# First four attention steps with the query-key projections one block ahead

## The chip, the cores and the metric

The kernel runs on one core of one Trainium2 chip. The metric is device time in microseconds (us) of one launch; "TensorE", "VectorE", "ScalarE" and "GpSimd" are PE, DVE, ACT and POOL in the rows of the profile, SP is the engine whose queue issues most transfers, and PEld is TensorE's loading of weights.

## The reference

One transformer layer on a sequence of 4096 tokens, width 256: banded attention with 16 heads of 16 columns, then a feed-forward block with binarised weights, each with a residual and a layer norm.

```python
q = _l2norm(proj(Wq)); k = _l2norm(proj(Wk)); v = proj(Wv)
attn = jnp.einsum('bhqd,bhkd->bhqk', q, k)
mask = (rel < 0) | (rel >= WINDOW)            # rel = key position - query position, WINDOW = 128
alibi = -jnp.abs(rel) * slopes[:, None, None]
attn = jax.nn.softmax(attn + where(mask, -1e30, alibi), axis=-1)
out = einsum('bhqk,bhkd->bhqd', attn, v) @ Wo
x = _layernorm(x + out)
h = gelu(x @ (alpha1 * sign(w1)).T + b1)      # alpha = mean |w| of a row
x = _layernorm(x + h @ (alpha2 * sign(w2)).T + b2)
```

## The kernel before

The tokens are cut into 32 blocks of 128. Attention works through the blocks in steps, one per block; step i handles the keys of block i, whose queries are those of blocks i and i-1. The work of one block passes through all engines, and every engine has its own program, written out by hand in order; semaphores tie them together. An engine works strictly in its written order, so a waiting instruction holds all that is behind it. Steps 0 to 3 are written out one by one (this is the head of the program, and all that is changed), steps 4 to 23 are a loop of four steps a turn, and the last eight steps run into the feed-forward block.

The names used here, each with its line in the rows:

- **qk(n)**: TensorE projects queries and keys of block n into a bank of PSUM (L430; block 0 at L499), float32, four passes of 512 columns. It waits until block n-2, which used the same bank, is normalised (`qkn_done`).
- **sq(n)** squares on ScalarE (L638), **sums(n)** on VectorE (L923), **seed(n)** on VectorE (L836); **norm(i)** is the pair logarithm and exponential on ScalarE (L643, L645) for block i+3; then a round of three short operations (L841, L843, L845) and the normalising of the rows (L946) on VectorE.
- **high(n)** on ScalarE (L652, L655) writes the float16 high halves of block n into `parts[n % 2]`; the low halves are subtracted on GpSimd (L1338, L1340); **double(n)** copies the query halves (on ScalarE, L665, in most steps; L898 on VectorE for the first blocks).
- **T(n)**: SP's queue issues a DMA transpose of `parts` into slot n % 4 of `qkT` (L284). high(n+2) overwrites the same half of `parts` and so waits until T(n) has landed.
- **S(i,c)**: TensorE's scores of step i, chunk c of four (L398). **E(i,c)**: ScalarE's exponential of that chunk (L685). S(i,c) needs E of two chunks earlier, since the chunks take two pairs of banks in turn.
- **cuts**: four per step on GpSimd (L1320), which set masked weights to zero.
- **v(n)**: TensorE's projection of the values (L441), then their fading by VectorE (L915). It is written into the bank that also holds the small normaliser parts of VectorE, so it waits for `newton` (a finished round) and `onorm_done` (a finished scaling of sums).
- **W(q)**: TensorE's weighted sums of block q (L420), in step q+2. VectorE turns them (L852), takes the reciprocal (L858) and scales (L861, `onorm_done`), and TensorE projects them with `wo` (L450).

TensorE's program opens with warm-up products of a constant (L492, `WARM`), and has two more such stretches in the head: 14 before step 0 (`WARM_AGAIN`) and 6 in step 1 (`WARM_BETWEEN`).

Of the kernel before, what the change touches and what calls it, by code (L numbers as in the profile page):

```python
# [15 lines left out]
P = 128  # L16
D = 256
# [28 lines left out]
WARM_AGAIN = 14  # L46

WARM_BETWEEN = 6


# [67 lines left out]
def build(nc, x, xT, wqkvT, woT, w1, w1T, b1c, w2T, b2, out):  # L118
    with ExitStack() as ctx:
# [81 lines left out]

        rden_in_psum = ps[:, VO, D + 192:D + 192 + H]
        parts_in_psum = tuple(ps[:, VO, D + 64 * n:D + 64 * n + 2 * H + 1] for n in range(3))

        def in_psum(i, next3):

            return next3 and (not isinstance(i, int) or i >= 0)
# [59 lines left out]
        def _(sp):  # L267
# [6 lines left out]
            def turn_parts(n, s):  # L274
# [6 lines left out]
                if isinstance(n, int) and n < 2:  # L281
                    sp.wait_ge(first_low, n + 1)
# [4 lines left out]
            for n in range(DC):  # L287
                sp.dma_start(wqkv[:, n, 0:2 * D], wqkvT[:, n, 0:2 * D]).then_inc(wqk_in[n], 16)
                sp.dma_start(xt[:, n], xT[n]).then_inc(x_in[n], 16)
            for n in range(DC, XS):  # L290
# [3 lines left out]
            load_block(XS, 0)  # L294
            turn_parts(0, 0)
            turn_parts(1, 1)
            turn_parts(2, 2)
            load_block(XS + 1, 1)
            load_block(XS + 2, 2)
            turn_parts(3, 3)  # L300
            sp.dma_start(wo[:], woT).then_inc(wo_in, 16)
            load_block(XS + 3, 3)
            for n in range(2):
                sp.dma_start(resid[:, n, :], x[n]).then_inc(first_resid[0], 16)
            turn_parts(XS, 0)
            for n in range(2, XS):
                sp.dma_start(resid[:, n, :], x[n]).then_inc(first_resid[1], 16)
# [64 lines left out]
        def _(pe):  # L372
# [187 lines left out]
            def means():  # L560

                pe.wait_ge(w2_summed, 3)
                pe.wait_ge(v_ready, NB)
                nc.tensor.matmul(mean_at, mean_ones[:], w2_sum[:], start=True, stop=True).then_inc(means_done, 1)
# [68 lines left out]
        def _(act):  # L633
# [34 lines left out]
            def step(i, slot, next2=True, next3=True, ln=True, both=True, norm=True, high_first=False,  # L668
                     squares_first=False, doubled=True, before_rows=None, amid=None, tail=None):
                par = slot % 2  # L670
                own, near = OWN_AT[slot], NEAR_AT[par]
                at = slice(near, own + 1, own - near)

                def exps(c):
                    act.wait_ge(s_done, i * NC + c + 1)
                    if c == 0:
                        count(act, pv_done, i - 2)
                    banks = ps[:, SC + 2 * (c % 2):SC + 2 * (c % 2) + 2, :]
                    if both:
                        to = prob[:, at, CH * c:CH * c + CH, :].rearrange("p s h q -> p h s q")  # L680
                        scored = banks.rearrange("p b (t s q) -> p (b t) s q", t=2, s=2)
                    else:
                        to = prob[:, own, CH * c:CH * c + CH, :]
                        scored = banks.rearrange("p b (t q) -> p (b t) q", t=2)[:, :, P:2 * P]
                    nc.scalar.activation(to, scored, ACT.Exp, scale=QK_SCALE ** -2).then_inc(exp_done, 1)  # L685

                if high_first:
                    high_halves(i + 2, par)
                exps(0)
                exps(1)  # L690
                if next2 and not high_first and not squares_first:
# [5 lines left out]
                if squares_first:  # L697
                    high_halves(i + 2, par)
                if amid:
                    amid()  # L700
                exps(2)
                exps(3)
                if norm and (next3 or ln):
                    norm_of(i, next3, ln)
                if next2 and doubled:
# [19 lines left out]

            nc.scalar.preload_act_table_set("natural_log_exp_and_others")
# [106 lines left out]
        def _(dve):  # L833
# [67 lines left out]
            def split_keys(n):  # L901

                dve.wait_ge(hi_done, n + 1)
                nc.vector.tensor_tensor(parts[:, n, H:2 * H, 2:4, :],
                                        qkn[:, n, D:2 * D].rearrange("p (h d) -> p h d", d=HD).unsqueeze(2).to_broadcast(
                                            [P, H, 2, HD]),
                                        parts[:, n, H:2 * H, 0:2, :], ALU.subtract).then_inc(first_low, 1)
                double(n, n)

            def fade_values(n, slot):  # L910

                dve.wait_ge(v_done, n + 1)
                count(dve, pv_done, n - 3)
                v = ps[:, VO, 0:D].rearrange("p (h d) -> p h d", d=HD)
# [115 lines left out]
            sums_of(1)  # L1030
# [459 lines left out]
```

## Time and profile before

| | us |
|---|---|
| median of 3 runs | 356.14 (355.18 to 356.33) |
| the profiled execution, its own time | 355.92 |
| its span, first to last instruction | 354.2 |
| TensorE busy | 333.9 (94%) |
| ScalarE busy | 295.4 (83%) |
| VectorE busy | 288.7 (81%) |
| GpSimd busy | 266.8 (75%) |

The span leaves out 1.72 us of the profiled execution's time. Busy shares are averages over stages that differ; the head, from 0 to 40.14 us, is the part that the change rewrites. "Idle before" in a row is the time that an engine stood still ahead of the row, with the instruction that ended it.

### The profile page before, as it was taken

The page shows a single profiled execution, that of the slowest core. Times are in us where ns is not written, and L with a number is a line of the kernel's source. Part 1 is how long each engine was busy: PE and PEld are TensorE (multiplying, and loading weights), DVE is VectorE, ACT ScalarE, POOL GpSimd, SP SyncE. Part 2 cuts the span into 40 slices and gives each one's busy share as a digit, 9 for nine tenths or more (in the row PEclk, how much of TensorE's full clock was granted, in tenths as well). Part 3 has the DMA queues.
Part 4 walks back from the last instruction along what each step waited for, and adds up shares of the span by engine and source line. Part 5 has one row for each costly group of instructions (what it writes and reads, how often), then busy time and mean ns, then how long its engine had stood idle before and what let it go on. Part 6 is the DMA issues. An engine that isn't in the chain of part 4 may idle for free.

```text
span 354.2 us, 12284 instructions
## 1 busy us (share of the span) xinstructions
PE 333.9 (94%) x4269; PEld 227.1 (64%) x4269; DVE 288.7 (81%) x763; ACT 295.4 (83%) x496; POOL 266.8 (75%) x314
## 2 busy tenths in 40 slices
PE   8798998999999999999998979898999999999991
PEld 6555675667666676676675657665766666676781
DVE  5875789789889989989987866988778788787785
ACT  2489988889989899899898996878788888897843
POOL 1149998888988998998899986856685765766343
PEclk9999999999999999999999998999999999999998
DMA  7577854555555565686775583012320721413113
GB/s 227 130 140 174 192 125 92 120 119 119 119 118 118 107 135 128 148 176 150 160 173 125 101 165 60 3 20 44 59 57 6 121 83 37 118 59 60 59 61 119
DMA packets 99489, 38.32 MB, mean 108 GB/s; under 512 B 84736, under 2 KB 98432, under 8 KB 99328
## 3 DMA queue, kind: packets, MB, share of 16 engines
q1 hardware_dynamic: 99456, 37.89, 48.3%
q8 instruction: 19, 0.31, 0.4%
q14 instruction: 14, 0.11, 0.1%
HBM read 12.72 MB, written 4.19 MB: 48 GB/s over the span
## 4 chain that ended last, share of the span: by engine, by line
PE 69%; DVE 10%; issue 6%; ACT 5%; DMA 4%; POOL 3%; SPq 1%; DVEq 1%; POOLq 0%; ACTq 0%
PE ps L551 14%; PE ps L581 13%; PE ps L430 11%; PE ps L420 11%; PE ps L441 6%; PE ps L398 6%; PE ps L450 5%; ACT prob L685 2%; DMA yT<-yparts 2%; DMA qkT<-parts 1%; SPq L284 1%; PE ps L492 1%; DMA resid<-in_x 1%; DVE otok L861 1%; POOL prob L1320 1%
## 5 line engine op out<-in xcount | busy, mean ns | idle before, releaser
L1320 POOL TENSOR_SCALAR_AFFINE_SELECT prob<-prob 128x1024 f32<-128x1024 f32 x126 | 133.7, 1094 | 5.9 <-ACT prob L685 5.7
L685 ACT ACTIVATE prob<-ps 128x1024 f32<-128x1024 f32 (+1 forms) x128 | 121.8, 1004 | 11.4 <-PE ps L398 11.1
L551 PE MATMUL ps<-yT,sgn 128*128 128x512 f16 x256 | 61.0, 379 | 2.5 <-DMA yT<-yparts 2.5
L430 PE MATMUL ps<-wqkv,xt 128*128 128x512 f32 x124 | 61.4, 617 | 1.2 <-DVE qkn L946 1.1
L420 PE MATMUL ps<-prob,faded 128*17 128x128 f32 x2016 | 61.2, 273 | 0.6 <-POOL prob L1320 0.6
L755 ACT ACTIVATE ps<-ps,bias,alpha 128x512 f32<-128x512 f32 x64 | 47.9, 749 | 15.3 <-PE ps L551 12.1
L420 PEld LDWEIGHTS ps<-prob,faded 128*17 128x17 f32 x2016 | 52.3, 97 | 6.5 <-issue 3.7
L1388 POOL TENSOR_TENSOR resid<-z,resid 128x256 f32 (+1 forms) x31 | 22.4, 724 | 29.4 <-DVE z L1148 29.4
L551 PEld LDWEIGHTS ps<-yT,sgn 128*128 128x128 f16 x256 | 24.7, 98 | 26.1 <-issue 3.1
L398 PE MATMUL ps<-qkT 64*64 64x192 f16 (+3 forms) x1024 | 36.8, 255 | 4.7 <-DMA qkT<-parts 2.2
L398 PEld LDWEIGHTS ps<-qkT 64*64 64x64 f16 x1024 | 20.9, 106 | 25.4 <-issue 25.1
L1340 POOL TENSOR_TENSOR parts<-qkn,parts 128x512 f16<-128x512 f32 x30 | 35.7, 1189 | 0.0
L441 PE MATMUL ps<-wqkv,xt 128*128 128x256 f32 x128 | 34.7, 395 | 0.8 <-DVE otok L861 0.8
L430 PEld LDWEIGHTS ps<-wqkv,xt 128*128 128x128 f32 x124 | 21.1, 189 | 21.5 <-issue 18.2
L1338 POOL TENSOR_TENSOR parts<-qkn,parts 128x256 f16<-128x256 f32 x30 | 20.3, 677 | 19.0 <-ACT parts L655 18.9
L450 PEld LDWEIGHTS ps<-wo,oT 128*128 128x128 f32 x112 | 21.4, 192 | 14.5 <-issue 12.8
L581 PE MATMUL ps<-sgn,w 128*128 128x256 f16 x256 | 30.6, 273 | 0.0
L450 PE MATMUL ps<-wo,oT 128*128 128x256 f32 x112 | 29.4, 386 | 0.6 <-DVE turned L852 0.6
L1370 POOL TENSOR_TENSOR yparts<-resid,yparts 128x256 f16<-128x256 f32 (+1 forms) x32 | 21.5, 689 | 11.0 <-ACT yparts L749 11.0
L581 PEld LDWEIGHTS ps<-sgn,w 128*128 128x128 f16 x256 | 25.0, 98 | 6.3
L441 PEld LDWEIGHTS ps<-wqkv,xt 128*128 128x128 f32 x128 | 23.6, 194 | 7.6 <-issue 4.3
L581 PE MATMUL ps<-sgn,prob 128*128 128x256 f16 x240 | 28.3, 273 | 0.0
(114 smaller groups left out, 558.6 us busy)
## 6 DMA issues: line engine op xcount, KB each, us to landing
xt<-in_xT SPq DMA_DIRECT2D x32, 128.0 KB, 2.3
resid<-in_x SPq DMA_DIRECT2D x32, 128.0 KB, 2.3
out_dram<-resid SPq DMA_DIRECT2D x7, 512.0 KB, 2.9
w<-in_w2T SPq DMA_DIRECT2D x1, 1024.0 KB, 8.2
w<-in_w1T SPq DMA_DIRECT2D x4, 256.0 KB, 3.3
w_nat<-in_w SPq DMA_DIRECT2D x4, 256.0 KB, 4.3
wqkv<-in_wqkvT SPq DMA_DIRECT2D x3, 256.0 KB, 4.1
qkT<-parts SPq DMA_TRANSPOSE x32, 4.3
```

The source lines that it names most:

```text
L398: mm = nc.tensor.matmul(ps[keys, SC + 2 * (c % 2) + hp, 2 * P * t + first:2 * P * t + last], qkT[row, H // 2 + 2 * c + t, slot, keys], moving,
L420: mm = nc.tensor.matmul(ps[32 * m:32 * m + HD + 1, OT, P * c:P * c + P], v, p, start=(n == 0), stop=(n == 1 or not near))
L430: mm = nc.tensor.matmul(ps[:, QK[slot % 2], :], xt[:, slot, k, :], wqkv[:, k, 0:2 * D], start=(k == 0), stop=(k == DC - 1))
L441: mm = nc.tensor.matmul(ps[:, VO, 0:D], xt[:, slot, k, :], wqkv[:, k, 2 * D:3 * D], start=(k == 0), stop=(k == DC - 1))
L450: mm = nc.tensor.matmul(ps[:, OT, D * par:D * par + D], oT[:, par, k, :], wo[:, k, :], start=(k == 0), stop=(k == DC - 1))
L551: mm = nc.tensor.matmul(ps[:, bank, :], sgn1[:, c, P * k:P * k + P], yT[:, par, a, c, :, :], start=(m == 0), stop=(m == 2 * DC - 1))
L581: mm = nc.tensor.matmul(ps[:, banks[b], 0:D], hid[par][:, a, k, P * b:P * b + P], sgn2[:, k, :], start=(m == 0), stop=(m == 2 * HC - 1))
L685: nc.scalar.activation(to, scored, ACT.Exp, scale=QK_SCALE ** -2).then_inc(exp_done, 1)
L755: nc.scalar.activation(bank, bank, ACT.Gelu, bias=bias1[:, k:k + 1], scale=alpha1[:, k:k + 1]).then_inc(gelu_done, 1)
L1320: return nc.gpsimd.affine_select(out=at, in_=at, compare_op=ALU.is_ge, fill=0.0, base=-near, pattern=[[0, 2 * CH], [1 if near else -1, P]] ...
L1340: nc.gpsimd.tensor_tensor(parts[:, par, H:2 * H, 2:4, :], src[:, H:2 * H, :].unsqueeze(2).to_broadcast([P, H, 2, HD]), parts[:, par, H:2 * ...
L1388: nc.gpsimd.tensor_tensor(resid[:, m, :], z[:, b, :], resid[:, m, :], ALU.add).then_inc(zsum, 1)
```

## The change

Only the head is changed. (1) TensorE does qk(3), v(1) and v(2) ahead of step 0 in place of 14 warm-up products, and the 6 products of step 1 are gone. The values of blocks 1 and 2 go into the bank of the weighted sums (`first_values`), which is free then. In steps 0, 1 and 2 TensorE does qk(4), qk(5), qk(6), a block ahead of before, and step 3 has none. (2) v(3) is in step 2 ahead of W(0), and v(4) in step 3, between the second and third chunk of the scores. (3) ScalarE does high(i+3) and norm(i+1) in step i, and nothing but exponentials in step 3. (4) Blocks 2 to 5 are doubled on VectorE. (5) The seeds of blocks 1 and 2 go to PSUM in place of SBUF. (6) The first block's transfer and the second half of the query-key weights are issued by ScalarE's queue. (7) On SP's queue the loads of blocks 5 and 6 stand between the transposes, each ahead of the next one. (8) The sums of `w2` come in four pieces.

```diff
-            def project_v(n, slot):
+            def first_value(n):
+                pe.wait_ge(x_in[n], 16)
+                for k in range(DC):
+                    mm = nc.tensor.matmul(first_values[n], xt[:, n, k, :], wqkv[:, k, 2 * D:3 * D],
+                                          start=(k == 0), stop=(k == DC - 1))
+                mm.then_inc(v_done, 1)
+            def project_v(n, slot, ahead=0):
...
-                if not isinstance(n, int) or 2 <= n < NB - 1:
-                    pe.wait_ge(newton, norm_base(n - 2, True) + NORM_OPS)
+                if not isinstance(n, int) or n < NB - 1:
+                    pe.wait_ge(newton, norm_base(n - 2 + ahead, True) + NORM_OPS)
                 count(pe, onorm_done, n - 3)
...
-            project_v(0, 0)
+            first_value(0)
             project_qk(2, 2)
-            pe.wait_ge(id_made, 2)
+            pe.wait_ge(consts, 1)
+            first_value(1)
+            project_qk(3, 3)
+            first_value(2)
             pe.wait_ge(consts, 2)
-            keep_warm(WARM_AGAIN, SC)
-            step(0, 0, out=False, pv=False, both=False, early=True)
-            step(1, 1, out=False, pv=False, behind=lambda: keep_warm(WARM_BETWEEN, OT))
-            step(2, 2, out=False, early=True)
-            step(3, 3, out=False, early=True)
+            for i in range(2):
+                for c in (0, 1):
+                    scores(i, c, i, i, i > 0)
+                project_qk(i + 4, i)
+                for c in (2, 3):
+                    scores(i, c, i, i, i > 0)
+            for c in (0, 1):
+                scores(2, c, 0, 2, True)
+            project_qk(6, 2)
+            for c in (2, 3):
+                scores(2, c, 0, 2, True)
+            project_v(3, 3, ahead=1)
+            for c in range(NC):
+                weighted_sum(0, c, 0)
+            for c in (0, 1):
+                scores(3, c, 1, 3, True)
+            project_v(4, 0, ahead=1)
+            for c in (2, 3):
+                scores(3, c, 1, 3, True)
+            for c in range(NC):
+                weighted_sum(1, c, 1)
...
+            act.dma_start(xt[:, 0], xT[0]).then_inc(x_in[0], 16)
+            act.dma_start(wqkv[:, 1, 0:2 * D], wqkvT[:, 1, 0:2 * D]).then_inc(wqk_in[1], 16)
             nc.scalar.preload_act_table_set("natural_log_exp_and_others")
...
-            step(0, 0, ln=False, both=False, high_first=True, doubled=False)
-            step(1, 1, ln=False, squares_first=True)
-            step(2, 2, ln=False, squares_first=True)
-            step(3, 3, ln=False, squares_first=True)
+            squares(3, 1)
+            high_halves(2, 0, first=True)
+            norm_of(0, True, False)
+            for i in range(3):
+                for c in (0, 1):
+                    exps(i, c, i, i > 0)
+                squares(i + 4, i % 2)
+                high_halves(i + 3, 1 - i % 2)
+                for c in (2, 3):
+                    exps(i, c, i, i > 0)
+                norm_of(i + 1, True, False)
+            for c in range(NC):
+                exps(3, c, 3)
...
             seeds_of(6, False)
+            turn_sums(0)
+            round_of(3, True, False)
+            normalise_rows(6, 0)
             scale_sums(0, 0)
```

TensorE, between block 2's projection and the first scores (L492 are the warm-up products; L422 is qk, L430 the new early values, L390 the scores). Before:

```order
L430 MATMUL ps<-wqkv,xt 128x512 [waits qkn_done,x_in_2]
L430 MATMUL ps<-wqkv,xt 128x512
L492 MATMUL ps<-mean_ones 128x128 [waits consts,id_made]
L492 MATMUL ps<-mean_ones 128x128 x13
L398 MATMUL ps<-qkT 64x64 [waits qk_in_even,consts]
```

And of the change:

```order
L422 MATMUL ps<-wqkv,xt 128x512 [waits qkn_done,x_in_2]
L422 MATMUL ps<-wqkv,xt 128x512
L430 MATMUL ps<-wqkv,xt 128x256 [waits x_in_1,consts]
L430 MATMUL ps<-wqkv,xt 128x256
L422 MATMUL ps<-wqkv,xt 128x512 [waits qkn_done,x_in_3]
L422 MATMUL ps<-wqkv,xt 128x512
L430 MATMUL ps<-wqkv,xt 128x256 [waits x_in_2]
L430 MATMUL ps<-wqkv,xt 128x256
L390 MATMUL ps<-qkT 64x64 [waits qk_in_even,consts]
```

One query-key and two value projections stand where the warm-up products stood.

TensorE in step 3, from its second chunk of scores to the weighted sums W(1). Before (L430 is qk(6), L441 is v(4), L420 is W(1)):

```order
L398 MATMUL ps<-qkT 64x192 [waits exp_done,consts]
L398 MATMUL ps<-qkT 64x192 x7
L430 MATMUL ps<-wqkv,xt 128x512 [waits qkn_done,x_in_2]
L430 MATMUL ps<-wqkv,xt 128x512
L398 MATMUL ps<-qkT 64x192 [waits exp_done,consts]
L398 MATMUL ps<-qkT 64x192 x7
L398 MATMUL ps<-qkT 64x192 [waits exp_done,consts]
L398 MATMUL ps<-qkT 64x192 x7
L441 MATMUL ps<-wqkv,xt 128x256 [waits onorm_done,newton,v_ready]
L441 MATMUL ps<-wqkv,xt 128x256
L420 MATMUL ps<-prob,faded 17x128 [waits cut_ready,sums_turned,v_ready]
L420 MATMUL ps<-prob,faded 17x128 x15
```

And of the change (L390 scores, L441 v(4), L412 W(1)):

```order
L390 MATMUL ps<-qkT 64x192 [waits exp_done,consts]
L390 MATMUL ps<-qkT 64x192 x7
L441 MATMUL ps<-wqkv,xt 128x256 [waits onorm_done,newton,v_ready]
L441 MATMUL ps<-wqkv,xt 128x256
L390 MATMUL ps<-qkT 64x192 [waits exp_done,consts]
L390 MATMUL ps<-qkT 64x192 x7
L390 MATMUL ps<-qkT 64x192 [waits exp_done,consts]
L390 MATMUL ps<-qkT 64x192 x7
L412 MATMUL ps<-prob,faded 17x128 [waits cut_ready,sums_turned,v_ready]
L412 MATMUL ps<-prob,faded 17x128 x15
```

v(4), with its wait for the scaling of block 0's sums, has moved ahead of the third and fourth chunk of the scores, and qk(6) is no longer there.

SP's queue around the first transposes, of the change (L268 and L269 load a block, L281 is a transpose; before, the three transposes stood together and the loads of blocks 5 and 6 behind them):

```order
L268 DMA xt<-in_xT 128x256 [waits v_done]
L269 DMA resid<-in_x 128x256
L281 DMA_TRANSPOSE qkT<-parts 128x16x128 [waits parts_ready,first_low,wv_in]
L268 DMA xt<-in_xT 128x256 [waits v_done]
L269 DMA resid<-in_x 128x256
L281 DMA_TRANSPOSE qkT<-parts 128x16x128 [waits parts_ready,first_low,wv_in]
```

Two loads now stand between T(0) and T(1), and two more between T(1) and T(2).

## Rows read from the trace of the kernel before

**Rows 1.** Windows by stage: length, then each engine's busy us and instruction count.

```profile
17.85:40.14 22.29, 21.27 (x301) 12.63 (x301) 14.89 (x32) 20.83 (x39) 17.67 (x19) 1.00 0.76 168
40.14:169.39 129.25, 127.45 (x2077) 86.93 (x2078) 114.17 (x311) 117.20 (x196) 117.96 (x118) 1.00 0.60 129
```

**Rows 2.** Chain that ended last, in order of time: start, length, what.

```profile
13.33 4.38 DMA qkT<-parts
...
34.66 1.91 PE ps L430 x4
...
37.17 1.06 PE ps L441 x4
38.23 1.87 PE ps L420 x64
...
40.14 0.63 PE ps L398 x16
...
59.74 1.02 issue
```

**Rows 3.** Timeline of TensorE up to step 0: start, length, engine, line, operation.

```profile
5.84 0.28 PEld L499 LDWEIGHTS ps<-wqkv,xt 128*128 128x128 f32 x1 [0.81 <-DMA wqkv<-in_wqkvT]
...
6.40 1.30 PE L499 MATMUL ps<-wqkv,xt 128*128 128x512 f32 x2
...
13.13 3.29 PE L492 MATMUL ps<-mean_ones 128*128 128x128 f32 x28
17.85 0.36 PE L398 MATMUL ps<-qkT 64*64 64x64 f16 x14 [1.43 <-DMA qkT<-parts]
```

**Rows 4.** Timeline of ScalarE, the first exponentials and step 2.

```profile
18.70 1.06 ACT L685 ACTIVATE prob<-ps 128x512 f32<-128x512 f32 x2
...
28.86 1.92 ACT L685 ACTIVATE prob<-ps 128x1024 f32<-128x1024 f32 x2
30.73 0.60 ACT L638 ACTIVATE sq<-ps 128x512 f32<-128x512 f32 x1
31.23 0.41 ACT L652 ACTIVATE parts<-qkn 128x256 f16<-128x256 f32 x1
...
32.05 1.93 ACT L685 ACTIVATE prob<-ps 128x1024 f32<-128x1024 f32 x2
33.86 0.20 ACT L643 ACTIVATE lnx<-ps 128x32 f32<-128x32 f32 x1
34.10 0.23 ACT L645 ACTIVATE rnorm<-lnx 128x32 f32<-128x32 f32 x1
34.23 0.61 ACT L665 ACTIVATE parts<-parts 128x512 f16<-128x512 f16 x1
34.75 1.92 ACT L685 ACTIVATE prob<-ps 128x1024 f32<-128x1024 f32 x2
```

**Rows 5.** SP's queue, and transposes' landing times, 12 to 30 and 30 to 200 us.

```profile
16.64 1.86 SPq L284 DMA_TRANSPOSE qkT<-parts  x1
...
23.80 1.15 SPq L271 DMA_DIRECT2D xt<-in_xT  x1
...
DMA to landing us min/median/max: 4.3/4.5/4.7
...
DMA to landing us min/median/max: 4.2/4.3/6.0
```

**Rows 6.** Timeline of VectorE: two seeds, and the turning and scaling of W(0).

```profile
11.83 0.61 DVE L836 TENSOR_SCALAR half<-ss 128x32 f32<-128x32 f32 x1
...
26.67 0.18 DVE L836 TENSOR_SCALAR ps<-ss 128x32 f32<-128x32 f32 x1
...
34.28 0.72 DVE L852 STREAM_TRANSPOSE turned<-ps 128x512 f32<-128x512 f32 x1 [1.11 <-PE ps L420]
...
36.48 0.42 DVE L861 TENSOR_TENSOR otok<-turned,ps 128x256 f32<-128x256 f32 x1
```

**Rows 7.** TensorE after its longest idle time, and window with its granted clock.

```profile
210.56 1.02 PE L551 MATMUL ps<-yT,sgn 128*128 128x512 f16 x4 [2.51 <-DMA yT<-yparts]
...
212.00:213.50 1.50, 1.50 (x5) 0.50 0.29 55
```

More of the change, by code:

```diff
@@ L44 @@
 WARM = 8
-WARM_AGAIN = 14
-WARM_BETWEEN = 6
+HEAD = 3
 OWN_AT, NEAR_AT = (2, 3, 4, 5), (0, 1)
@@ L205, in in_psum @@
         def in_psum(i, next3):
-            return next3 and (not isinstance(i, int) or i >= 0)
+            return next3 and (not isinstance(i, int) or i > -HEAD)
         def root_parts(i, next3):
@@ L666, in double @@
                                      ACT.Copy).then_inc(parts_ready, 1)
-            def step(i, slot, next2=True, next3=True, ln=True, both=True, norm=True, high_first=False,
-                     squares_first=False, doubled=True, before_rows=None, amid=None, tail=None):
-                par = slot % 2
[L671 to L691, printed above, removed]
@@ new lines, in exps @@
+            def exps(i, c, slot, both=True):
+                own, near = OWN_AT[slot], NEAR_AT[slot % 2]
+                at = slice(near, own + 1, own - near)
+                act.wait_ge(s_done, i * NC + c + 1)
+                if c == 0:
+                    count(act, pv_done, i - 2)
+                banks = ps[:, SC + 2 * (c % 2):SC + 2 * (c % 2) + 2, :]
+                if both:
+                    to = prob[:, at, CH * c:CH * c + CH, :].rearrange("p s h q -> p h s q")
+                    scored = banks.rearrange("p b (t s q) -> p (b t) s q", t=2, s=2)
+                else:
+                    to = prob[:, own, CH * c:CH * c + CH, :]
+                    scored = banks.rearrange("p b (t q) -> p (b t) q", t=2)[:, :, P:2 * P]
+                nc.scalar.activation(to, scored, ACT.Exp, scale=QK_SCALE ** -2).then_inc(exp_done, 1)
@@ L696, in step @@
                     before_rows()
-                if squares_first:
-                    high_halves(i + 2, par)
                 if amid:
                     amid()
-                exps(2)
-                exps(3)
-                if norm and (next3 or ln):
+                exps(i, 2, slot)
+                exps(i, 3, slot)
+                if next3 or ln:
                     norm_of(i, next3, ln)
-                if next2 and doubled:
+                if next2:
                     double(i + 2, par)
@@ L1342, in low_halves, with step @@
                                         parts[:, par, H:2 * H, 0:2, :], ALU.subtract).then_inc(lo_done, 1)
-            def step(i, slot, next2=True, both=True, low_at=1, behind=None):
+            def step(i, slot, next2=True, both=True, low_at=1, ahead=0, behind=None):
                 for pair in range(NC // 2):
                     if next2 and pair == low_at:
-                        low_halves(i + 2, slot % 2)
+                        low_halves(i + 2 + ahead, (slot + ahead) % 2)
                     cut_pair(i, pair, slot, both)
@@ L1350, in step @@
                     behind()
-            for n in range(2):
+            for n in range(HEAD):
                 pool.wait_ge(first_high, n + 1)
-                nc.gpsimd.tensor_tensor(parts[:, n, 0:H, 1, :], qkn[:, n, 0:D].rearrange("p (h d) -> p h d", d=HD),
-                                        parts[:, n, 0:H, 0, :], ALU.subtract).then_inc(lo_done, 1)
-            step(0, 0, both=False, low_at=0)
-            step(1, 1, low_at=0)
-            for n in range(2, 5):
-                step(n, n % XS, low_at=0)
+                nc.gpsimd.tensor_tensor(parts[:, n % 2, 0:H, 1, :], qkn[:, n % 2, 0:D].rearrange("p (h d) -> p h d", d=HD),
+                                        parts[:, n % 2, 0:H, 0, :], ALU.subtract).then_inc(lo_done, 1)
+            step(0, 0, both=False, ahead=1)
+            step(1, 1, ahead=1)
+            step(2, 2, ahead=1)
+            step(3, 3, next2=False)
+            step(4, 0, low_at=0)
             with pool.Fori(0, (NB - 12) // XS) as t:
```

69 lines of the change are left out of this document (38 added, 31 removed).

## The prediction

> **What bounds the kernel now.** I read the windows by stage first, then the chain of work that ended last, then each engine's timeline over the head. The windows show two full engines in the head: from the first scores at 17.85 to step 4 at 40.14, TensorE is busy 21.27 of 22.29 us and ScalarE 20.83; in the loop behind it TensorE is busy 127.45 of 129.25 us [rows 1]. The chain runs through TensorE there, line after line without a gap [rows 2]. So the loop keeps TensorE's pace, and the head is worth what it moves the start of step 4, which stands at 40.14. Everything behind is the same program; a shift of step 4 passes to the end.
>
> ScalarE explains the head's pace: in step 2 it starts a pair of exponentials at 28.86 and, without a pause, the next step's at 34.75. By differences of starts a pair of E is 1.87 (1.81 the second), sq 0.50, high 0.82 (31.23 to 32.05), norm 0.37 (33.86 to 34.23) and double 0.52 [rows 4]: 5.89 a step. TensorE's own list for a step is also near 5.9: qk(6) 1.91, v(4) 1.06, W(1) 1.87, and the 0.60 left between the first two for a pair of scores [rows 2]; two such pairs and that make 6.0, less where a pair overlaps its neighbours.
>
> **The change part by part.**
>
> *Early projections.* qk(3), v(1), v(2) are 1.91 + 2 x 1.06 = 4.0 us, and replace warm-up products that began at 13.13; the first transpose lands at 13.33 + 4.38 = 17.71 [rows 2, 3]. There are 4.6 us; qk(3) must wait for block 1's normalising (I take 14.6, an estimate: 1.4 us behind the start of the warm-up products, whose place v(1) takes), so the last ends near 17.5. It fits, with 0.2 to spare, and costs nothing; if it ran over, step 0 would start later by as much. It takes 4 us and 20 warm-up products out of TensorE behind 17.85, which makes about 15 of its 21 us needed. TensorE then no longer bounds the head, ScalarE does, if nothing stops it.
>
> *First loads on two queues.* The second weight half lands at 5.84, while the pass that uses it starts at 6.40, in the engine's own pace [rows 3]. An earlier landing is worth 0; a later first load costs at most one issue, under 0.5. I take 0. The Trainium skill (DMA: Bandwidth & Descriptors, Issuing engines are not separate DMA queues) says that both queues end on the same transfer engines and only issue time is saved; by it too the edit is worth 0, at most the issue time, and that is hidden.
>
> *Seeds to PSUM.* A seed into SBUF took 0.61, one into PSUM 0.18 [rows 6]; twice 0.43 on VectorE's opening chain. I expect 0.15 to 0.3 of it at block 2's normalising. T(1), next, takes it back.
>
> *Loads between transposes.* A transpose holds SP's queue 1.86, the load behind one takes 1.15, and a landing comes 4.3 to 4.7 after issue [rows 5]. T(0) issued at 13.2 (13.33, less the seed's gain), the two loads (1.15 + 0.4) end near 16.8, so T(1) is issued 0.2 later than its 16.64 and behind 256 KB of loads; I take its landing at 21.3, with 20.9 (no loss) and 22.0 as ends. high(3) is now ahead of E(0,2) and waits for T(1).
>
> *ScalarE's walk.* norm(0) is now ahead of E(0,0), which goes from 18.70 to 18.9. E pair to 19.9; sq(4) waits for qk(4), 20.1; high(3) at 21.35 (T(1)); E(0,2) 22.2; norm(1) 23.2; E(1,0) 23.55; sq(5) waits for qk(5) (S(1,1) behind E(0,3), then 1.91), 25.6; high(4) 26.1; E(1,2) 26.95; norm(2) 28.75; E(2,0) 29.15; sq(6) 31.25, again behind qk(6); high(5) 31.75; E(2,2) 32.55; norm(3) 34.4 to 34.85. So step 2's exponentials start at 29.15 where they started at 28.86: ScalarE has a block more of preparation behind it, and no lead. The lead should be paid out in step 3, which has only four E, 3.75 in place of 5.89.
>
> *The step's new wait.* TensorE: qk(6) 29.3 to 31.2, S(2,2) and S(2,3), v(3), then W(0) 32.9 to 34.8, S(3,0) and S(3,1) to 35.2. Then v(4), which waits for W(0) to be scaled. From the start of the turning to the end of the scaling was 34.28 to 36.90, 2.62 us, with the round and the normalising of a block between [rows 6]; the same rows stand between them now. Turned at 34.87, scaled at 37.5, v(4) from 37.6 to 38.7. Before, TensorE had qk(6) and S(3,2), S(3,3) to do in that time; now these chunks stand behind v(4), and E(3,2), ready for 36.7, starts at 39.1. Then a pair of S, for which I take 0.5, W(1) 39.15 to 41.0, and S(4,0) at 41.05 against 40.14: **+0.9 us**. What is late next is only step 4 itself; ScalarE ends E(3,3) at 41.1 and is not late for it.
>
> *Doubling on VectorE.* ScalarE saves 0.52 in steps 1 to 3. VectorE has the time: it is busy 14.89 of 22.29 [rows 1]; blocks 3 and 4 are doubled while it waits for squares. If VectorE had no room, each copy would cost up to its 0.6. GpSimd's list is the same in sum, and its cuts of block 1 and 2 are ready before W(0) and W(1) by my count, the second by 1.5 us. The sums of w2 in four pieces lie in VectorE's pauses: 0.
>
> **Sum.** Profiled execution 355.92 (span 354.2) + 0.9 = 356.8; its time is 0.22 below the median 356.14, so against the runs it is 357.0. The bounds: T(1) on time and no wait of sq behind qk gives back at most 1.35 of ScalarE's path, which puts S(4,0) at 39.7 (-0.45, 355.7); T(1) at 22.0 gives +1.6 (357.7).
>
> **The rivals.**
>
> *Wait not met.* The scaling of W(0) is done before S(3,1) ends, as it would be if norm(3) came 1.7 us earlier than in my walk. Then v(4) is free, S(3,2) comes at once, and step 4 follows ScalarE: norm(3) plus four E, S(4,0) near 37.9, 2.2 us earlier: 353.9. For it speaks the 4 us taken from TensorE; against it that ScalarE has only 1.4 us of pauses in my walk. It decides at W(0)'s turning: under 33.2 us it is this one.
>
> *Clock.* My walk leaves TensorE idle from 20.5 to 22.7, 26.2 to 28.0 and 35.2 to 37.6 (1.8 to 2.4 us), with the warm-up products gone. In the trace, 2.51 us without products at 208 were followed by a granted clock of 0.50, 1.2 GHz, at 212 [rows 7]; the 1.43 us ahead of step 0 [rows 3] by none. A stretch at half clock of about 3 us loses half of it: +1.6 more, 358.6. The Trainium skill (TensorE: Matmul & The Clock Gate, Part 1) has the throttled state as the default and activity as what releases it, and warns of kernels whose waits let the clock fall again and again; by that page warm-up products are not free to remove, and the sum would be this rival's. The trace agrees in kind.
>
> *Transposes late.* T(1) or T(2) lands in up to 6.0, the longest seen [rows 5], since loads stand ahead of them: high(3) at 22.8, all +1.5: 358.0.
>
> *Stall behind goes.* Step 7's scores waited 1.02 at 59.74 [rows 2] for a transpose, the one of 6.0. With another phase of the transfers it may vanish: 357.0 - 1.0 = 356.0.
>
> **How the numbers follow.** Mine 0.50, wait not met 0.15, clock 0.15, late transposes 0.10, stall gone 0.10. A measurement of this kernel tells about 0.3%, 1.07 us, from no change: below 355.07 faster, above 357.21 slower. My case's value is close below that edge; a third of it lies above. Slower: 0.17 + 0.15 + 0.08 = 0.40; faster: 0.15 and 0.03 of the last, 0.18; same 0.42. The range runs from 354.7 to 358.6: it leaves out most of the first rival and the far end of the clock, takes in both bounds of T(1). My own case's range is 355.7 to 357.7.
>
> **What would show it.** Right: step 2's E starts between 28.5 and 29.6; a TensorE wait of about 2 us in front of v(4) ended by the scaling (VectorE's `otok`), and a ScalarE wait of 2 us in front of E(3,2); S(4,0) at 40.7 to 41.4. Wrong: no such wait; high(3) not ended by T(1); passes of qk of double length behind a pause; or a time that moves while S(4,0) stands where I say, which would put the cause into the loop.

## The result

| | before | change |
|---|---|---|
| median, us | 356.23 (355.18 to 356.41, 6 runs) | 358.31 (354.96 to 358.88, 6 runs) |
| ratio | | 1.0066, 95% interval 1.0037 to 1.0094 |
| profiled execution, its own time | 355.92 | 354.96 |
| its span | 354.2 | 352.8 |

The change is slower by 0.7%. The profiled execution of the change is the fastest of its six; the other five lie between 358.0 and 358.9. Its profile is read here for what happens in the head, and a second one (`after_again`, below) is nearer to the usual execution.

TensorE in the head of the change (timeline: start, length, engine, line, operation, and idle time before with what ended it; L422 is qk, L430 an early value, L390 scores, L441 v, L412 W, L492 warm-up):

```profile
4.50 1.96 PE L499 MATMUL ps<-wqkv,xt 128*128 128x512 f32 x4
6.29 1.88 PE L422 MATMUL ps<-wqkv,xt 128*128 128x512 f32 x4
...
16.82 0.42 PE L390 MATMUL ps<-qkT 64*64 64x64 f16 x16 [0.65 <-DMA qkT<-parts]
...
21.57 0.85 PE L390 MATMUL ps<-qkT 64*64 64x192 f16 x16 [2.08 <-ACT prob L701]
22.35 1.98 PE L422 MATMUL ps<-wqkv,xt 128*128 128x512 f32 x4
...
26.85 0.36 PE L390 MATMUL ps<-qkT 64*64 64x192 f16 x8 [2.06 <-ACT prob L701]
...
28.05 3.68 PE L422 MATMUL ps<-wqkv,xt 128*128 128x512 f32 x4
...
37.95 1.60 PE L441 MATMUL ps<-wqkv,xt 128*128 128x256 f32 x4 [2.38 <-DVE otok L886]
...
40.26 2.67 PE L412 MATMUL ps<-prob,faded 128*17 128x128 f32 x64
42.87 0.63 PE L390 MATMUL ps<-qkT 64*64 64x256 f16 x16
```

Step 4's first scores, S(4,0), start at 42.87, where they started at 40.14 [rows 2]. TensorE's stretches that matter for this are the three with an idle time of 2 us ahead of them, and what follows each. The three idle times of the prediction's walk are there, 2.08, 2.06 and 2.38 us, and behind two of them the same operations take longer: qk(6) takes 3.68 where qk(5) takes 1.98, v(4) 1.60 where an undisturbed one takes 1.1, W(1) 2.67 against 1.94 in the timeline of before. The windows of TensorE say why (length, busy us and count, granted clock, DMA share, GB/s):

```profile
17.85:40.14 22.29, 15.10 (x196) 0.88 0.67 145
...
27.50:29.00 1.50, 1.24 (x10) 0.72 0.82 208
29.00:30.50 1.50, 1.50 (x3) 0.50 0.09 24
...
32.00:38.00 6.00, 3.62 (x97) 1.00 0.74 166
38.00:39.50 1.50, 1.50 (x8) 0.64 0.02 5
39.50:41.00 1.50, 1.50 (x33) 0.50 0.26 68
41.00:42.50 1.50, 1.50 (x48) 0.73 0.85 197
```

TensorE was busy 21.27 us of the first window before [rows 1], and is busy 15.10 now: the work did leave. But the granted clock in the head, 1.00 before, falls twice to 0.50, the lower of the two levels (1.2 GHz).

ScalarE over the same time (L701 exponentials, L657 squares):

```profile
20.01 0.42 ACT L671 ACTIVATE parts<-qkn 128x256 f16<-128x256 f32 x1 [0.22 <-DVE qkn L973]
...
27.87 1.92 ACT L701 ACTIVATE prob<-ps 128x1024 f32<-128x1024 f32 x2
31.77 0.60 ACT L657 ACTIVATE sq<-ps 128x512 f32<-128x512 f32 x1 [1.98 <-PE ps L422]
...
35.46 1.94 ACT L701 ACTIVATE prob<-ps 128x1024 f32<-128x1024 f32 x2
40.07 1.94 ACT L701 ACTIVATE prob<-ps 128x1024 f32<-128x1024 f32 x2 [2.67 <-PE ps L390]
```

The slow qk(6) reaches ScalarE as a wait of 1.98 ahead of sq(6), and the wait ahead of v(4) as one of 2.67 ahead of E(3,2). high(3), at 20.01, was released by the normalising, not by the landing of T(1).

Although step 4 comes 2.73 later, this execution's span is 1.4 shorter than that of before. To compare executions I split each time into four: the opening up to the start of qk(1), the head from there to S(4,0), the rest up to the end of the span, and the time outside the span.

| profiled execution | opening | head | rest | outside | own time |
|---|---|---|---|---|---|
| before | 7.54 | 32.60 | 314.06 | 1.72 | 355.92 |
| change | 6.29 | 36.58 | 309.93 | 2.16 | 354.96 |
| change, again | 6.90 | 37.98 | 309.92 | 2.27 | 357.07 |

The opening differs because the first pass over the weights takes a different time in each execution: L499's four products took 3.01 in the profile of before and 1.96 in this one. The profile's clock column reads 1.00 there, so a lower clock in the opening would be a guess from these lengths alone. The difference does not belong to the change: qk(1) starts at 7.54, 7.53 and 6.67 in the three profiles of the kernel before and its variants, and between 6.29 and 7.64 in those of the change and its own. The head is 3.98 longer. The rest is 4.13 shorter, and the views of both name most of that. The list of TensorE's waits between 45 and 160 us has, for the kernel before (engine, line, releaser: us in total, times, longest):

```profile
PE ps L398 <- issue: 1.0, 1, 1.0
PE ps L441 <- DVE otok L861: 0.8, 2, 0.4
```

and nothing at all for the change. The stall at 59.74 [rows 2] and two waits for the scaling of sums are gone: 1.8 us. The other piece is the first transpose of the feed-forward block, which the prediction had used only as a sample of an idle TensorE [rows 7]. In the profile of the change:

```profile
209.84 1.02 PE L570 MATMUL ps<-yT,sgn 128*128 128x512 f16 x4 [0.67 <-DMA yT<-yparts]
```

That wait was 2.51 [rows 7] and is 0.67; the transfer lands 4.7 us after its issue instead of 6.4, which is another 1.8. No slow stretch follows either: from this product to the next weighted sums it is 3.13 us in place of 4.76. The pieces named so far come to 3.6 of the 4.13, so that of these 1.6 us only 0.5 are left at the end; where the other 1.1 are lost again was not traced.

### The profile page after: what moved, and what is told of

The parts are those of the page before. It is cut to its first block, busy times and chain, and to the rows that moved or that the text cites. A ratio compares the mean times of both kernels' runs of the same rounds, so it can differ in the third digit from the quotient of the medians.

```text
span 352.8 us, 12203 instructions
## 1 busy us (share of the span) xinstructions
PE 330.2 (94%) x4229; PEld 222.1 (63%) x4229; DVE 291.2 (83%) x768; ACT 294.0 (83%) x493; POOL 265.5 (75%) x313
## 4 chain that ended last, share of the span: by engine, by line
PE 73%; DVE 9%; ACT 6%; issue 4%; POOL 3%; DMA 3%; DVEq 0%; POOLq 0%; ACTq 0%; SPq 0%
PE ps L570 15%; PE ps L600 13%; PE ps L412 12%; PE ps L422 12%; PE ps L390 6%; PE ps L441 6%; PE ps L450 5%; ACT prob L701 3%; DMA yT<-yparts 1%; DMA qkT<-parts 1%; POOL prob L1355 1%; ACT parts L674 1%; PE ps L492 1%; DVE turned L877 1%; POOL parts L1375 1%
## 5 line engine op out<-in xcount | busy, mean ns | idle before, releaser
L701 ACT ACTIVATE prob<-ps 128x1024 f32<-128x1024 f32 (+1 forms) x128 | 121.7, 1004 | 10.6 <-PE ps L390 10.1
L422 PE MATMUL ps<-wqkv,xt 128*128 128x512 f32 x124 | 63.0, 632 | 1.5 <-DVE qkn L973 1.5
L412 PE MATMUL ps<-prob,faded 128*17 128x128 f32 x2016 | 62.2, 275 | 0.1
L412 PEld LDWEIGHTS ps<-prob,faded 128*17 128x17 f32 x2016 | 52.8, 98 | 6.3 <-issue 3.0
L1424 POOL TENSOR_TENSOR resid<-z,resid 128x256 f32 (+1 forms) x31 | 22.4, 725 | 29.6 <-DVE z L1183 29.6
L390 PE MATMUL ps<-qkT 64*64 64x192 f16 (+3 forms) x1024 | 37.0, 256 | 7.5 <-ACT prob L701 6.0
L390 PEld LDWEIGHTS ps<-qkT 64*64 64x64 f16 x1024 | 21.1, 106 | 29.1 <-issue 29.1
L422 PEld LDWEIGHTS ps<-wqkv,xt 128*128 128x128 f32 x124 | 21.5, 192 | 22.3 <-issue 18.9
L1375 POOL TENSOR_TENSOR parts<-qkn,parts 128x512 f16<-128x512 f32 x29 | 34.3, 1183 | 0.0
L441 PE MATMUL ps<-wqkv,xt 128*128 128x256 f32 x116 | 31.2, 392 | 2.4 <-DVE otok L886 2.4
L1373 POOL TENSOR_TENSOR parts<-qkn,parts 128x256 f16<-128x256 f32 x29 | 19.5, 672 | 15.7 <-ACT parts L674 15.4
L877 DVE STREAM_TRANSPOSE turned<-ps 128x512 f32<-128x512 f32 x32 | 22.9, 717 | 5.9 <-PE ps L412 5.6
```

The source lines that it names most:

```text
L390: mm = nc.tensor.matmul(ps[keys, SC + 2 * (c % 2) + hp, 2 * P * t + first:2 * P * t + last], qkT[row, H // 2 + 2 * c + t, slot, keys], moving,
L412: mm = nc.tensor.matmul(ps[32 * m:32 * m + HD + 1, OT, P * c:P * c + P], v, p, start=(n == 0), stop=(n == 1 or not near))
L422: mm = nc.tensor.matmul(ps[:, QK[slot % 2], :], xt[:, slot, k, :], wqkv[:, k, 0:2 * D], start=(k == 0), stop=(k == DC - 1))
L441: mm = nc.tensor.matmul(ps[:, VO, 0:D], xt[:, slot, k, :], wqkv[:, k, 2 * D:3 * D], start=(k == 0), stop=(k == DC - 1))
L877: nc.vector.transpose(turned[:].rearrange("p b d -> p (b d)"), ps[:, OT, :]).then_inc(sums_turned, 1)
L1375: nc.gpsimd.tensor_tensor(parts[:, par, H:2 * H, 2:4, :], src[:, H:2 * H, :].unsqueeze(2).to_broadcast([P, H, 2, HD]), parts[:, par, H:2 * ...
```

## The experiments

Eleven runs of ten kernels follow (`fill_again` repeats `fill`, and `after_again` the change), each with the kernel before beside it on the same chip; the medians of before were 355.45, 355.57 and 355.86 in the three sets. "Fillings" are warm-up products of a constant, written into a bank of PSUM that is free at that time; the rows count two matmuls to a product.

**`fill`, `fill_again`: TensorE busy in the three gaps**, by six, eight and nine products.

```diff
                 for c in (2, 3):
                     scores(i, c, i, i, i > 0)
+                pe.wait_ge(qkn_done, i + 4)
+                keep_warm((6, 8)[i], QK[1 - i])
...
+            pe.wait_ge(qkn_done, 6)
+            keep_warm(9, QK[1])
             project_v(4, 0, ahead=1)
```

> The changed kernel with warm-up products put into TensorE's three idle stretches of the head: 6 behind S(0,3), 8 behind S(1,3), 9 ahead of v(4). Theory (the clock): the two drops to 0.50 in the head go, qk(6) takes 1.98 in place of 3.68 and v(4) to W(1) 3.5 in place of 5.1; S(4,0) comes at 39.5 to 41.1 in place of 42.87, and the median falls by 2 to 3.3 from 358.3, to 355 to 356.3. Rival (the order of v(4), or the transfers, cost the time and the clock costs nothing): the products only fill idle time, median 358.3 again, within 0.5.

Measured: 354.93 (353.67 to 355.36, 12 runs), ratio 0.9984 (0.9969 to 0.9998). Repeated in the third set:

> The change with the three fillings of warm-up products a second time, as the ground for the next two. If the fillings give back what the lower clock cost, it stands where it stood, at 354.9, 0.2% under the kernel before, with the first scores of step 4 near 40.2. If that value came from a lucky phase of the transfers, it comes out near 355.7, where its neighbours stood.

Measured: 354.87 (353.65 to 355.32, 11 runs), ratio 0.9968 (0.9954 to 0.9981). TensorE in the profile of `fill_again`:

```profile
6.46 1.88 PE L422 MATMUL ps<-wqkv,xt 128*128 128x512 f32 x4
...
20.20 1.60 PE L492 MATMUL ps<-mean_ones 128*128 128x128 f32 x12 [0.53 <-DVE qkn L977]
...
25.07 2.05 PE L492 MATMUL ps<-mean_ones 128*128 128x128 f32 x16
...
28.40 1.98 PE L422 MATMUL ps<-wqkv,xt 128*128 128x512 f32 x4
...
34.16 2.27 PE L492 MATMUL ps<-mean_ones 128*128 128x128 f32 x18
36.61 1.10 PE L441 MATMUL ps<-wqkv,xt 128*128 128x256 f32 x4 [0.17 <-DVE otok L890]
...
39.96 0.63 PE L390 MATMUL ps<-qkT 64*64 64x256 f16 x16
```

The warm-up products do no work of the kernel and every wait for data is still there, yet qk(6) is back at 1.98 and v(4) at 1.10, and the granted clock is 1.00 from 14 to 45 us in both profiles. The head is 33.50 (33.35 in `fill`). So of the change's head, 36.58 and 37.98, 3.1 to 4.6 us were the lower clock, and against before's 32.60 there remain 0.75 and 0.90. Of that the time gets 3.3, in part because the wait for the feed-forward block's transpose is 2.2 again in both profiles with fillings, where the change has 0.7.

This does not rest on single profiles. The record gives every execution's mean granted clock: 0.976 to 0.979 in eleven of the twelve executions of the change and 0.985 in the fast one that was profiled first, against 0.990 to 0.994 in all 23 with the three fillings.

**`fill12`: the first two gaps filled, not the third.** The diff is that of `fill` without its last two lines.

> The changed kernel with warm-up products in the first two idle stretches only (6 behind S(0,3), 8 behind S(1,3)), none ahead of v(4). If each idle stretch of 2 us or more loses the clock by itself: the drop behind v(4) stays and costs 1.6, median 1.3 to 1.9 above the kernel with all three fillings (354.93). If the drops come from the sum of idle time in the head: no drop left, the same as with all three.

Measured: 357.11 (355.6 to 359.1, 12 runs), ratio 1.0056 (1.0033 to 1.0079). The gap ahead of v(4) alone, 2.38 us, is followed by a slow stretch:

```profile
37.44 1.95 PE L441 MATMUL ps<-wqkv,xt 128*128 128x256 f32 x4 [2.38 <-DVE otok L888]
...
40.09 2.33 PE L412 MATMUL ps<-prob,faded 128*17 128x128 f32 x64
42.36 0.63 PE L390 MATMUL ps<-qkT 64*64 64x256 f16 x16
```

The median is 2.2 above that of `fill`, where 1.3 to 1.9 was expected of a fall that stays. The head (34.89) shows 1.4 to 1.5 of it; behind step 4 this profile has waits of 0.8 and 0.7 in the loop that `fill` has not. The median also stands between two groups: six executions took 355.6 to 356.6 and six 357.6 to 359.1, and three of the slower six, the profiled one among them, have no lower mean clock (0.990) than the faster (0.988 to 0.989). So only the head's 1.4 to 1.5 is shown to be the clock.

**`after_again`: the change once more**, for a profile that isn't the fastest run.

> The changed kernel once more, beside the others of this set, for a second profile and its spread: 357.5 to 359, with clock drops in the head; if the first profiled execution (354.96) was the rule, 355.

Measured: 358.12 (357.07 to 358.72, 6 runs), ratio 1.008 (1.0059 to 1.0101). TensorE:

```profile
22.28 1.02 PE L390 MATMUL ps<-qkT 64*64 64x192 f16 x16 [2.17 <-ACT prob L701]
23.23 3.42 PE L422 MATMUL ps<-wqkv,xt 128*128 128x512 f32 x4
...
30.54 3.78 PE L422 MATMUL ps<-wqkv,xt 128*128 128x512 f32 x4
...
41.52 1.10 PE L441 MATMUL ps<-wqkv,xt 128*128 128x256 f32 x4 [2.38 <-DVE otok L886]
...
44.88 0.63 PE L390 MATMUL ps<-qkT 64*64 64x256 f16 x16
```

Here the first gap has its slow stretch too, and the third has none. Two of the three gaps are followed by one in each of the two profiles, not the same two; those hit behind the first or second cost a whole qk at half clock. With a later opening as well (6.90 against 6.29) this is 2.0 us of span above the first profile. It is the fastest of its six executions, but its mean clock, 0.979, is that of the others (0.976 to 0.979). By these profiles and the two of `fill`, one slow stretch costs the head 1.4 to 3 us, since what stands behind the qk can be slow too, as v(3) with 1.79 here.

**`v4last`, `fill_v4last`: the wait for the scaling out of the way.** v(4) moves behind W(1); in the second with the fillings (4 products ahead of S(3,2) in place of 9 ahead of v(4)).

```diff
             for c in (0, 1):
                 scores(3, c, 1, 3, True)
-            project_v(4, 0, ahead=1)
             for c in (2, 3):
                 scores(3, c, 1, 3, True)
             for c in range(NC):
                 weighted_sum(1, c, 1)
+            project_v(4, 0, ahead=1)
```

> The changed kernel with v(4) moved behind W(1), nothing else. Theory (v(4)'s wait for the scaling of W(0) holds the scores behind it): TensorE's wait of 2.4 and ScalarE's of 2.7 in step 3 go, S(4,0) comes 1.5 to 2.5 earlier than 42.87, and with the idle stretch the second drop of the clock may go too: median 355 to 356.8. Rival (the clock alone is the loss, TensorE waits for exponentials and cuts anyway): S(4,0) within 0.5 of 42.87, median 358 within 0.5.

Measured: 357.72 (357.17 to 358.47, 6 runs), ratio 1.0067 (1.0048 to 1.0087): by the ratios no faster than the change, and not the 355 to 356.8 that the theory wanted. S(4,0) starts at 44.46, not earlier than 42.87.

> Both: warm-up products in the first two idle stretches and 4 ahead of S(3,2), and v(4) behind W(1). If clock and wait are two separate losses: S(4,0) at 37.5 to 39, median 353 to 354.5, below the kernel before. If they are one loss seen twice: the same median as the better of the two alone.

Measured: 355.72 (355.13 to 357.02, 12 runs), ratio 1.0019 (1.0005 to 1.0032). Expected were 353 to 354.5 if clock and wait are two separate losses, and the median of the better of the two alone if they are one; it came out 0.8 above `fill`. The wait for `otok` is gone in the head of both. `v4last` leaves other gaps, and the clock falls behind them: W(1), behind idle times of 1.05 and 0.56, takes 3.59. With fillings the head is 32.87, 0.5 to 0.6 shorter than with the wait, and no shorter than before; the rest of its span, 312.6, is longer than that of `fill` (311.3; 312.3 in `fill_again`), and has waits of 0.4 and 0.3 in the loop. TensorE in `fill_v4last`:

```profile
37.45 1.94 PE L412 MATMUL ps<-prob,faded 128*17 128x128 f32 x64
39.32 1.13 PE L441 MATMUL ps<-wqkv,xt 128*128 128x256 f32 x4
40.38 0.63 PE L390 MATMUL ps<-qkT 64*64 64x256 f16 x16
```

v(4) can't start before the scaling (36.6 in `fill_again`), and W(1) and one or the other chunk of the scores can't either, since they follow ScalarE. So 3 us of TensorE's work stand between that moment and S(4,0) in both orders, and the work taken from TensorE earlier leaves idle time that neither order fills. That is argued from the rows, not shown; an order with v(4)'s bank freed was not tried.

**`before_nofill`: the kernel before without its warm-up products in the head.**

```diff
             pe.wait_ge(consts, 2)
-            keep_warm(WARM_AGAIN, SC)
             step(0, 0, out=False, pv=False, both=False, early=True)
-            step(1, 1, out=False, pv=False, behind=lambda: keep_warm(WARM_BETWEEN, OT))
+            step(1, 1, out=False, pv=False)
```

> The kernel before without its 14 and 6 warm-up products in the head. Theory (idle TensorE loses its clock, products are what kept it in the head): a granted clock of 0.50 appears between 14 and 35 us, 0.5 to 3.5 us slower than before. Rival (the kernel before has too little idle time in its head for that): within 0.5 of before, and the clock stays 1.00 in the head.

Measured: 356.0 (353.63 to 356.85, 12 runs), ratio 1.0011 (0.9993 to 1.0028). TensorE:

```profile
16.98 0.64 PE L398 MATMUL ps<-qkT 64*64 64x64 f16 x16 [4.54 <-DMA qkT<-parts]
17.55 3.78 PE L430 MATMUL ps<-wqkv,xt 128*128 128x512 f32 x4
```

The same thing happens to the old order: 4.54 us idle, then qk(3) at half clock; the granted clock is 0.50 from 16 to 20. Its head is 35.08, 2.5 longer than with the products. The median is not apart from before's (0.5 above it, with an interval that takes in no change), at the low end of the 0.5 to 3.5 expected. The profiled execution took 354.21 and is the second fastest of its twelve; ten of the others have a mean clock of 0.974 to 0.982, lower than its 0.986. In it the rest of the span is 310.65, nearly as short as the change's: the stall at 59.74 is gone and the wait for the feed-forward block's transpose is 0.70, while the waits for the scaling of sums are not (1.1 us in the loop).

**`before_two_queues`, `fill_one_queue`: the first loads.** The edit of ScalarE's queue put alone into the kernel before, and taken out of `fill`.

```diff
+            act.dma_start(xt[:, 0], xT[0]).then_inc(x_in[0], 16)
+            act.dma_start(wqkv[:, 1, 0:2 * D], wqkvT[:, 1, 0:2 * D]).then_inc(wqk_in[1], 16)
```

> The kernel before with only its first loads on two queues. As above: 0 to 0.4 slower if nothing is gained inside the span, 0.3 to 0.8 faster if the second weight half is what qk(0) waits for.

Measured: 355.97 (354.8 to 356.48, 12 runs), ratio 1.0005 (0.999 to 1.002), qk(1) at 7.53 and a head of 32.65, against 7.54 and 32.60.

> The changed kernel with all three fillings, but with the first loads all on SP's queue as before. If the two queues are worth nothing at the start: median as with all three fillings, within 0.3, or 0.4 faster, since the time outside the span is 2.2 with ScalarE's queue and 1.7 without. If they let the first projection start earlier: 0.3 to 0.8 slower.

Measured: 355.72 (355.25 to 357.22, 12 runs), ratio 1.0015 (1.0 to 1.0029). That is 0.8 above `fill`, the size that the second theory names; but its qk(1), at 7.13, stands within the spread of the openings, so that an earlier first projection is not shown to be the cause. Its profile is of the slowest of the twelve executions (357.22) and has a late transpose. SP's queue, then ScalarE's high(4):

```profile
20.53 2.95 SPq L281 DMA_TRANSPOSE qkT<-parts  x1
```

```profile
27.27 0.42 ACT L677 ACTIVATE parts<-qkn 128x256 f16<-128x256 f32 x1 [1.18 <-DMA qkT<-parts]
```

T(2) lands 6.7 us after its issue, and high(4), the one that needs T(2), waits 1.18 for it. In `fill_again` T(2) is issued at 19.82, holds the queue for 1.64 and lands 5.3 after its issue, and high(4) does not wait for it. Whether the late landing comes from the queues or from its phase against the other transfers stays open; it is one profile.

**`fill_seeds_sbuf`: the seeds of blocks 1 and 2 in SBUF, as before.** `i > -HEAD` becomes `i >= 0` in `in_psum`.

> The fillings, with the seeds of blocks 1 and 2 (and the small parts of their rounds) in SBUF as before the change. Theory A, the one of the prediction: a seed costs 0.43 us more on VectorE's opening chain, 0.15 to 0.3 of it shows at the normalising, and the next transpose or wait takes it back, so the first scores of step 4 move by less than 0.3 and the time by less than 0.3. Theory B: nothing takes it back, since every step of the opening stands on VectorE's chain; the head is longer by 0.4 to 0.9 us, and so is the time, 355.4 to 355.8.

Measured: 355.11 (354.44 to 356.44, 12 runs), ratio 0.9979 (0.9964 to 0.9993), 0.24 above `fill_again`. VectorE, the seed of block 1 and what follows it, in `fill_seeds_sbuf` and then in `fill_again`:

```profile
10.94 0.55 DVE L865 TENSOR_SCALAR half<-ss 128x32 f32<-128x32 f32 x1
11.41 0.68 DVE L934 TENSOR_TENSOR parts<-qkn,parts 128x512 f16<-128x512 f32 x1
...
12.88 0.69 DVE L977 TENSOR_TENSOR qkn<-ps,rnorm 128x512 f32<-128x512 f32 x1
```

```profile
10.80 0.19 DVE L865 TENSOR_SCALAR ps<-ss 128x32 f32<-128x32 f32 x1
11.12 0.75 DVE L934 TENSOR_TENSOR parts<-qkn,parts 128x512 f16<-128x512 f32 x1
...
12.67 0.69 DVE L977 TENSOR_TENSOR qkn<-ps,rnorm 128x512 f32<-128x512 f32 x1
```

A seed into PSUM is 0.36 shorter, but the next instruction starts only 0.15 sooner behind the seed's start (0.32 for 0.47) and is 0.07 longer. From seed to normalising it is 1.87 against 1.94, so 0.07 a block is won, and S(4,0) stands 33.50 behind qk(1) against 33.47: nothing.

**`fill_loads_behind`: the loads of blocks 5 and 6 behind the third transpose, as before.**

```diff
-            for n in range(HEAD):
-                load_block(XS + n, n)
-                turn_parts(n, n)
+            load_block(XS, 0)
+            for n in range(HEAD):
+                turn_parts(n, n)
+            load_block(XS + 1, 1)
+            load_block(XS + 2, 2)
```

> The fillings, with the loads of blocks 5 and 6 behind the third transpose, as before the change. Theory A: the loads between the transposes make them late (the term of the prediction that had T(1) land at 21.3); without them the transposes land 0.3 to 1 us earlier and the time falls by up to 0.5. Theory B: the transposes land in time either way, and it is block 5's load that matters: behind T(2), issued near 19.5, it lands near 23, where the projection of block 5 wants it at 22.96, so TensorE waits there by 0 to 1 us and the time rises by as much.

Measured: 360.13 (359.76 to 360.42, 5 runs), ratio 1.0113 (1.0094 to 1.0133), 5.3 above `fill_again`; the head of its profile, 37.59, is 4.1 longer. SP's queue (the first row merges three transposes and the pauses between them), then TensorE:

```profile
13.35 8.31 SPq L281 DMA_TRANSPOSE qkT<-parts  x3
21.72 1.06 SPq L268 DMA_DIRECT2D xt<-in_xT  x1
```

```profile
26.88 3.07 PE L424 MATMUL ps<-wqkv,xt 128*128 128x512 f32 x4 [3.41 <-DMA resid<-in_x]
```

The 8.31 us run from the issue of T(0) to the end of T(2)'s. The transposes themselves hold the queue for 1.42, 1.94 and 1.84 of them; in the other 3.1 the queue stands still, at the head of its order a transpose whose halves are not yet written (T(1) goes at 16.59, T(2) at 19.82). With the loads between them, the loads go largely in these pauses: T(2) is issued 13.4 behind qk(1) in `fill_again` and 12.2 here. Here block 5's load, behind T(2) in order, is issued at 21.72, and qk(5) waits 3.41 for it (the profile names the load beside it) and then runs at the lower clock. That is theory B in kind, but it had the wait at 0 to 1 us, with T(2) out of the way near 19.5. A projection a block ahead needs its load a block ahead.

## Why the prediction was right or wrong

The forecast was 357.0 within 354.7 to 358.6; 358.3 is inside, 1.3 above the value, and on the slower side. Its own case was not the one that happened, and that the value comes so near is partly luck: 3.3 us of lower clock were left out, and so were the waits behind the head that went away. By its steps:

- **The walk and its idle times: right.** The opening is no part of the forecast, so its times are moved with it. Counted from an opening that came 1.25 earlier, the idle times were due from 19.2, 24.9 and 33.9, of 2.2, 1.8 and 2.4 us. The first two stand where they should with 2.08 and 2.06; the third, behind the slow qk(6), is 2.38 long. Step 2's exponentials, due at 29.15, so 27.90, start at 27.87. With the clock held up the walk is right to its end: in `fill_again` S(4,0) stands 33.50 behind qk(1), which from before's opening (7.54) is 41.04, where the walk had 41.05.
- **"The step's new wait", +0.9: right in size, and in cause for most of it.** v(4) waits for the scaling, E(3,2) 2.67 with it; turning to scaling took 2.61 us, 2.62 in the prediction. With the clock held up by fillings, the head is 0.75 and 0.90 longer than before. Taking the wait away brings back 0.5 to 0.6 of that.
- **The clock: the step that failed.** The sum "355.92 + 0.9 = 356.8" priced the three idle times at nothing, and the rival "Clock" got 0.15. It is what happened: `fill` against the change is 354.9 against 358.1 to 358.3, about 3.3 us. That rival's price, 1.6 for one stretch, was mis-sized by half, since two of the three gaps are followed by a slow stretch. The argument for a low chance was a row with 2.51 us idle followed by a fall and one of 1.43 followed by none [rows 3, 7], and 1.8 to 2.4 lies between, so the rows gave no ground for a price of nothing. The Trainium skill (TensorE: Matmul & The Clock Gate, Part 1) takes the throttled state as the default and activity as what lifts it; `fill` agrees, with 3.3 us for 46 matmuls of whose results the kernel uses nothing.
- **Early projections cost nothing: right.** They end 0.65 us before the first transpose lands, which S(0,0) waits for as before (1.43 then). It stands 10.53 behind qk(1), 10.31 before; the transpose lands 4.7 after its issue in place of 4.4.
- **T(1) late: right in time, nearly a tie in cause.** It was to land at 21.3 and let high(3) go at 21.35, 13.81 us behind qk(1). It landed at 19.9 (4.5 after its issue at 15.36), 0.1 ahead of the end of the normalising, and high(3) went at 20.01, 13.72 behind qk(1), released by the normalising. In `after_again` (13.81) and `fill_again` (13.90) it was released by T(1), as predicted. T(1) was issued 9.07 behind qk(1), 9.10 before; with the loads behind the transposes (`fill_loads_behind`) it is 8.95, and it lands 13.3 behind qk(1) in place of 13.6 to 13.9, so the loads ahead of it cost tenths. What that edit does for qk(5), whose load would else stand behind T(2) (+5.3), was missing in the prediction.
- **Seeds, 0.15 to 0.3 and eaten: eaten, and smaller,** 0.07 a block.
- **First loads on two queues, 0: right** alone in the kernel before (ratio 1.0005); inside the change it stays open, see `fill_one_queue`.
- **Doubling on VectorE, 0: nearly.** A copy took 1.04 beside GpSimd's cuts, and 0.28 to 0.55 elsewhere in the profile, but behind the long one VectorE had 2.06 us of pause.
- **Nothing behind the head changes: wrong.** "A shift of step 4 passes to the end" missed 1.8 us of waits in the loop, and 1.8 ahead of the feed-forward block's first product, that the change does not have. The rival "Stall behind goes" had 1.0 of it. For the medians the sum would have been +0.9 for the order, -1.8 for the loop, +0.4 outside the span, which is -0.5 and what `fill` measured (-0.5 and -1.0), and +3.3 for the clock: +2.8, where 2.1 and 2.55 were measured. The 3.3 is itself the difference between `fill` and the change, so this orders the parts after the fact and proves none.
- **"Wait not met": did not happen.** The turning of W(0) stood at 35.19, not under 33.2.
- **Its signs.** The two waits of its own case came. S(4,0) at 42.87 is outside its 40.7 to 41.4, by the clock, and step 2's E at 27.87 outside 28.5 to 29.6, by the opening. Two of its signs of being wrong came: high(3) not ended by T(1) (in the first profile), and a qk of nearly double length behind a pause.
- **Two slips in the working** that move neither the value nor the range. Of the 20 warm-up products "behind 17.85" 14 stood ahead of it (13.13 to 16.42). And "all +1.5: 358.0" for late transposes should be 358.5, since 1.5 is added to 357.0.

What stays open: why the time outside the span is 2.12 to 2.27 in the change and all its variants and 1.72 to 1.81 in the kernel before and its own. It isn't ScalarE's queue: `fill_one_queue` has 2.12, `before_two_queues` 1.75. Which part of the new head removes the waits of the loop is open too; `before_nofill` loses the stall as well, so it is not one edit of the change. The start of step 4 alone does not decide it either: at 40.18 in `before_two_queues` the stall of 1.0 is there, at 40.23 in `fill` it is not, and at 42.36 in `fill12` there is one of 0.7.

`fill` is the best version measured: 354.9 twice, 0.5 us under the kernel before in the first set and 1.0 in the third. It owes that to the waits that are gone behind the head, not to a shorter head: that is still 0.75 to 0.90 longer than before.

## What to carry to other kernels

Work that is taken from an engine that was full leaves idle time, and behind an idle time of 2 us on TensorE the lower clock cost 1.4 to 3 us of the head here, where a query-key projection takes 1.98: put something in its place, or price each gap by the row of this kernel nearest to it. Moving an instruction ahead moves its wait ahead too, so list what is queued behind it, and move its load first. And another start of a long loop can remove or make a stall further on; compare the lists of waits behind the edit before crediting the edit.

## What was not expected of the hardware

- Idle times of 2.06 to 2.38 us were followed by the lower clock in some executions and not in others: the 2.08 in the first profile of the change by none, the 2.17 at the same place in the second by a qk of 3.42 in place of 1.98.
- Two idle times of 1.05 and 0.56 with little work between them were enough in `v4last`, where the 3.59 of W(1) follows.
- The same holds at the end. Nine of the thirteen profiles have a wait of 2.2 to 2.5 for the feed-forward block's transpose; a fall followed in six and none in three. It was followed by no fall in `fill` (clock 1.00 from 209 to 213) and by one in `fill_again`:

```profile
209.00:213.00 4.00, 4.00 (x26) 0.57 0.44 81
```

- The opening is as variable: L499 took 1.93 to 3.11 us over the profiles of all these kernels, 1.2 us that no edit of theirs explains.
- A transpose of the same size held SP's queue for 1.4 to 3.1 us: 1.42, 1.94 and 1.84 in `fill_loads_behind`, 1.42, 2.88 and 1.41 with loads between them in the change, 3.10 for T(1) in `fill_again`.
